# Gate's inner layer and logits, tile by tile in the stage before the gate

## The reference

```python
x = x + _L1_gnn_ref(xn, ...) + _L1_mix_ref(xn[None], ...)[0]          # attention over edges, token mix
x = x + _L1_ffn_ref(_layernorm(x, axis=-1)[None], L1_ffn_gw1, L1_ffn_gb1, L1_ffn_gw2, L1_ffn_gb2, ...)[0]
# the gate inside _L1_ffn_ref, for each row v of the normalised x:
#   hidden = relu(v @ gw1 + gb1)        512 -> 256
#   logits = hidden @ gw2 + gb2         256 -> 8
#   softmax over the 8, the 2 largest chosen and weighted; each row goes through its 2 experts (512 -> 1024 -> 512)
```

## Time and profile before

| | us |
|---|---|
| runs | 2231.5 median of 3, 2230.55 to 2233.77 |
| profiled execution | 2237.73, its span 2236.0 |
| PE busy in the span | 1948.7 (87%) |
| DVE busy | 1317.6 (59%) |
| POOL busy | 773.0 (35%) |
| ACT busy | 738.9 (33%) |
| mean granted clock of PE | 0.936 |

### The profile page before, as it was taken

How to read it: one execution, slowest core, us unless ns; L and a number is a source line. 1 busy time by engine, 2 the same in 40 slices (tenths; PEclk the granted TensorE clock), 3 DMA queues, 4 the chain that set the end, 5 groups by cost and what they waited for, 6 DMA issues and landing times. The chain is left out here.

```text
span 2236.0 us, 31082 instructions
## 1 busy us (share of the span) xinstructions
PE 1948.7 (87%) x10042; PEld 1082.3 (48%) x10043; DVE 1317.6 (59%) x3824; ACT 738.9 (33%) x1743; POOL 773.0 (35%) x849
## 2 busy tenths in 40 slices
PE   7998888988988988978769897699999884999997
PEld 4343433433433433433134453377777544777675
DVE  5883398898988988988753053176666423111111
ACT  0011244444444444443221130056666320222221
POOL 0000277777777777777700000011111000212211
PEclk9998998989999999999979898899999985999999
DMA  4001299999999999999930083355532142343451
GB/s 157 12 24 73 89 401 400 386 407 400 391 404 391 401 405 397 393 399 398 403 134 0 17 247 106 111 177 147 148 113 89 53 175 89 109 113 109 124 175 28
DMA packets 142939, 480.28 MB, mean 215 GB/s; under 512 B 16607, under 2 KB 17279, under 8 KB 142561
## 3 DMA queue, kind: packets, MB, share of 16 engines
q0 software_dynamic: 99952, 353.16, 41.9%
q1 hardware_dynamic: 42864, 125.60, 16.9%
HBM read 446.58 MB, written 32.11 MB: 214 GB/s over the span
## 5 line engine op out<-in xcount | busy, mean ns | idle before, releaser
L489 POOL DMA_INDIRECT m_ring<-in_table,m_rows_at x640 | 651.9, 1019 | 258.6 <-issue 144.1
L854 PE MATMUL m_acc<-m_ring,m_diag 64*64 64x512 f32 x2560 | 424.4, 675 | 129.5 <-ACT m_diag L663 129.5
L549 DVE CUSTOM_DVE_ANT_0 m_ring<-m_ring,m_coming,m_part 128x512 f32<-128x512 f32 x640 | 442.3, 747 | 43.0 <-DMA m_ring<-in_table,m_rows_at 33.5
L854 PEld LDWEIGHTS m_acc<-m_ring,m_diag 64*64 64x64 f32 x2560 | 136.1, 145 | 382.6 <-ACT m_diag L663 288.5
L663 ACT ACTIVATE m_diag<-m_eye,m_inner 128x64 f32<-128x64 f32 x640 | 222.3, 348 | 278.8 <-DVE m_inner L549 278.7
L1921 PEld LDWEIGHTS e_psU<-e_rowsT,x_w 128*128 128x128 f32 x1472 | 170.5, 194 | 14.2 <-issue 14.2
L1404 DVE CUSTOM_DVE_ANT_0 a_prob<-a_psS,xnT 128x1250 f32<-128x1250 f32 x80 | 116.8, 1460 | 102.3 <-PE a_psS L1341 102.3
L1921 PE MATMUL e_psU<-e_rowsT,x_w 128*128 128x128 f32 x1472 | 171.0, 278 | 3.0 <-DMA x_w<-in_we 1.9
L1930 PE MATMUL e_psY<-x_w,e_hT 128*128 128x512 f32 x368 | 161.7, 592 | 0.0
L1341 PE MATMUL a_psS<-a_k,a_q 128*128 128x512 f32 (+1 forms) x480 | 116.6, 379 | 20.7 <-DMA a_k<-qk_parts 16.3
L1327 POOL DMA_DIRECT2D a_q<-qk_parts x80 | 43.0, 539 | 257.5 <-PE a_psS L1341 257.1
(11 more groups left out here) (327 smaller groups left out, 2649.8 us busy)
## 6 DMA issues: line engine op xcount, KB each, us to landing
x_w<-in_we SPq DMA_DIRECT2D x16, 2048.0 KB, 11.0
xnT<-edge_log_counts SPq DMA_DIRECT2D x40, 640.0 KB, 3.9
m_ring<-in_table,m_rows_at POOLq DMA_INDIRECT x640, 6.7
qk_parts<-p_parts SPq DMA_DIRECT2D x32, 320.0 KB, 4.0
a_k<-qk_parts SPq DMA_DIRECT2D x32, 320.0 KB, 9.6
edge_log_counts<-p_log_cnt SPq DMA_DIRECT2D x10, 640.0 KB, 6.2
a_q<-qk_parts POOLq DMA_DIRECT2D x80, 64.0 KB, 2.1
edge_counts<-cnt SPq DMA_DIRECT2D x10, 320.0 KB, 2.1
```

The lines of the kernel that those rows point to most:

```text
L489: pool.indirect_dma_start(ring[:, slot, :], None, ins["table"], bass.IndirectOffsetOnAxis(rows_at[:, h, k:k + 1], 0)).then_inc(s_land[slot ...
L549: dve.tensor_tensor_reduce(ring[:, slot, 0:D], ring[:, slot, 0:D], coming[:, t % 2, :], part[:, b, k:k + 1], 0.0, ALU.mult, ALU.add, inner ...
L854: mm = pe.matmul(acc[to, i, :], diag[rows, h % 2 * TOPK + k, :], ring[rows, nth % RING, D:2 * D], start=h == 0 and k < 2, stop=h == HEADS ...
```

## The change

The gate's inner layer, its Relu, its logits and the addition of their bias move from the start of stage_gate into the loops of stage_join, one tile at a time: Relu(t-3) at the end of ACT's iteration t, logits(t-4) and hidden(t-3) at the end of PE's iteration t, the logits' bias of tile t-5 in DVE's iteration t, behind var and ahead of the rows. psG is now two halves of one tile and psL one tile of 8 columns, each a single buffer. `logit` is a tensor that outlives the join. stage_gate begins with the maximum. The renumbering of psL's parts in stage_gate and the passing on of `gate` and `logit` are left out below.

```diff
@@ stage_join, scalar
-            for t in range(NT + 2):
+            for t in range(NT + 3):
...
-                if t >= 2:
+                if 2 <= t < NT + 2:
                     act.wait_ge(s["norm_turned"], t - 1)
                     act.activation(c.xnT[:, :, (t - 2) * P:(t - 1) * P], psN[:, t % 2, :].rearrange("p (k n) -> p k n", k=KC),
                                    ACT.Copy).then_inc(s["norm_out"], 1)
+                if t >= 3:
+                    u = t - 3
+                    act.wait_ge(s["hidden"], u + 1)
+                    if u >= 2:
+                        act.wait_ge(s["logits"], u - 1)
+                    for m in range(2):
+                        act.activation(gT[:, u % 2, m, :], psG[:, m, :], ACT.Relu, bias=gb1[:, m:m + 1]).then_inc(s["relu"], 1)
@@ stage_join, tensor
+            def hidden(u):
+                if u == 0:
+                    pe.wait_ge(s["ahead"], 16 * len(ahead))
+                else:
+                    pe.wait_ge(s["relu"], 2 * u)
+                pe.wait_ge(s["norm_out"], u + 1)
+                for m in range(2):
+                    for k in range(KC):
+                        mm = pe.matmul(psG[:, m, :], gw1[:, k, m * P:(m + 1) * P], c.xnT[:, k, u * P:(u + 1) * P],
+                                       start=k == 0, stop=k == KC - 1)
+                mm.then_inc(s["hidden"], 1)
+
+            def logits(u):
+                pe.wait_ge(s["relu"], 2 * u + 2)
+                if u:
+                    pe.wait_ge(s["logit_out"], u)
+                for m in range(2):
+                    mm = pe.matmul(psL[:, :], gT[:, u % 2, m, :], gw2[:, m, :], start=m == 0, stop=m == 1)
+                mm.then_inc(s["logits"], 1)
+
             turn(0)
-            for t in range(NT + 2):
+            for t in range(NT + 4):
...
-                if t >= 2:
+                if 2 <= t < NT + 2:
...
+                if t >= 4:
+                    logits(t - 4)
+                if 3 <= t < NT + 3:
+                    hidden(t - 3)
@@ stage_join, vector
-            for t in range(NT + 1):
+            for t in range(NT + 5):
...
                     dve.tensor_scalar(var[:, t:t + 1], mv[:, t, 1:2], EPS, None, ALU.add).then_inc(s["var"], 1)
-                if t >= 1:
+                if t >= 5:
+                    dve.wait_ge(s["logits"], t - 4)
+                    dve.tensor_tensor(logit[:, t - 5, :], psL[:, :], gb2[:, :], ALU.add).then_inc(s["logit_out"], 1)
+                if 1 <= t <= NT:
@@ stage_gate, tensor
-            for m in range(2):
-                for i, (a, n) in enumerate(CHUNKS):
-                    u = 3 * m + i
-                    if u >= 2:
-                        pe.wait_ge(s["relu"], u - 1)
-                    for k in range(KC):
-                        mm = pe.matmul(psG[:, u % 2, 0:n], gw1[:, k, m * P:(m + 1) * P], c.xnT[:, k, a:a + n],
-                                       start=k == 0, stop=k == KC - 1)
-                    mm.then_inc(s["hidden"], 1)
-            pe.wait_ge(s["relu"], 6)
-            for t in range(NT):
-                for m in range(2):
-                    mm = pe.matmul(psL[:, 0, t, :], gT[:, m, t * P:(t + 1) * P], gw2[:, m, :], start=m == 0, stop=m == 1)
-            mm.then_inc(s["logits"], 1)
@@ stage_gate, scalar
-            for m in range(2):
-                for i, (a, n) in enumerate(CHUNKS):
-                    u = 3 * m + i
-                    act.wait_ge(s["hidden"], u + 1)
-                    act.activation(gT[:, m, a:a + n], psG[:, u % 2, 0:n], ACT.Relu, bias=gb1[:, m:m + 1]).then_inc(s["relu"], 1)
@@ stage_gate, vector
-            dve.wait_ge(s["logits"], 1)
-            dve.tensor_tensor(logit[:, :, :], psL[:, 0, :, :], gb2[:, :].unsqueeze(1).to_broadcast([P, NT, EXP]), ALU.add)
-            dve.drain()
```

More of the change, by code:

```diff
@@ L1479, in _, with stage_join @@
                 message(g, 0, 4)
-def stage_join(c, msg, weights, ahead):
+def stage_join(c, msg, weights, gate, ahead):
     nc = c.nc
@@ L1491, in stage_join @@
         stats, mv, var, root, rstd = sb("stats", [P, NT, 6]), sb("mv", [P, NT, 2]), sb("var", [P, NT]), sb("root", [P, NT]), sb("rstd", [P, NT])
+        gw1, gw2, gb1, gb2, logit = gate
+        gT = sb("gT", [P, 2, 2, P])
         psT, psO, psN = ps("psT", [P, 2, D]), ps("psO", [P, 2, D]), ps("psN", [P, 2, D])
+        psG, psL = ps("psG", [P, 2, P]), ps("psL", [P, EXP])
         s = {n: c.sem("j_" + n) for n in ("turned", "mT", "out", "sum_out", "var", "root", "rows", "norm_turned", "norm_out",
-                                          "saved0", "saved1", "started", "ahead")}
+                                          "hidden", "relu", "logits", "logit_out", "saved0", "saved1", "started", "ahead")}
         block = st.enter_context(nc.Block())
@@ L1580, in _, with stage_attention @@
                                       ALU.subtract, ALU.mult).then_inc(s["rows"], 1)
-def stage_attention(c, ahead):
+def stage_attention(c, gate, ahead):
     ins = c.ins
@@ L1605, in stage_attention @@
         c.end_stage()
-        stage_join(c, msg, join, ahead)
+        stage_join(c, msg, join, gate, ahead)
         c.end_stage()
@@ L1617, in rows_of, with stage_gate @@
     return P if t < NT - 1 else TAIL
-def stage_gate(c, route, weights, ahead):
+def stage_gate(c, route, logit, ahead):
     nc, ins = c.nc, c.ins
@@ L1631, in stage_gate @@
         ps = lambda n, s: st.enter_context(nc.psum_tensor("r_" + n, s, F32))
-        gw1, gw2, gb1, gb2 = weights
-        gT = sb("gT", [P, 2, NP])
-        logit, expo, gate = sb("logit", [P, NT, EXP]), sb("expo", [P, NT, EXP]), sb("gate", [P, NT, EXP])
+        expo, gate = sb("expo", [P, NT, EXP]), sb("gate", [P, NT, EXP])
         peak, total, top, top_at = sb("peak", [P, NT]), sb("total", [P, NT]), sb("top", [P, NT, 8]), sb("top_at", [P, NT, 8], U32)
@@ L1649, in stage_gate @@
         hot_lane, hot_block = sb("hot_lane", [P, 2, NT, P]), sb("hot_block", [P, CHOICES, 2, NT, BLOCKS])
-        psG, psL, psK = ps("psG", [P, 2, D]), ps("psL", [P, 3, NT, EXP]), ps("psK", [P, 2, BLOCKS])
-        s = {n: c.sem("r_" + n) for n in ("iota", "number", "hidden", "relu", "logits", "shifted", "exp", "gap", "exp2",
+        psL, psK = ps("psL", [P, 2, NT, EXP]), ps("psK", [P, 2, BLOCKS])
+        s = {n: c.sem("r_" + n) for n in ("iota", "number", "shifted", "exp", "gap", "exp2",
                                           "tri", "both", "member", "ranked", "hot_block", "hot_lane", "listed", "blank", "blanked",
@@ L1693, in _ @@
         def _(pe):
-            for m in range(2):
-                for i, (a, n) in enumerate(CHUNKS):
-                    u = 3 * m + i
-                    if u >= 2:
-                        pe.wait_ge(s["relu"], u - 1)
-                    for k in range(KC):
-                        mm = pe.matmul(psG[:, u % 2, 0:n], gw1[:, k, m * P:(m + 1) * P], c.xnT[:, k, a:a + n],
-                                       start=k == 0, stop=k == KC - 1)
-                    mm.then_inc(s["hidden"], 1)
-            pe.wait_ge(s["relu"], 6)
-            for t in range(NT):
-                for m in range(2):
-                    mm = pe.matmul(psL[:, 0, t, :], gT[:, m, t * P:(t + 1) * P], gw2[:, m, :], start=m == 0, stop=m == 1)
-            mm.then_inc(s["logits"], 1)
             pe.wait_ge(s["tri"], 1)
             pe.wait_ge(s["member"], 1)
-            pe.matmul(psL[:, 1, :, :], below[:, :], member[:, :, :], start=True, stop=True)
-            pe.matmul(psL[:, 2, :, :], ones[:, :], member[:, :, :], start=True, stop=True).then_inc(s["ranked"], 1)
+            pe.matmul(psL[:, 0, :, :], below[:, :], member[:, :, :], start=True, stop=True)
+            pe.matmul(psL[:, 1, :, :], ones[:, :], member[:, :, :], start=True, stop=True).then_inc(s["ranked"], 1)
             pe.wait_ge(s["hot_block"], 1)
@@ L1771, in _ @@
             dve.wait_ge(s["ranked"], 1)
-            dve.tensor_copy(tally[:, :, :], psL[:, 2, :, :])
+            dve.tensor_copy(tally[:, :, :], psL[:, 1, :, :])
             dve.memset(before[:, 0, :], 0.0)
@@ L1795, in _ @@
             dve.tensor_scalar(base[:, :], start[:, 0:EXP], float(P), None, ALU.mult)
-            dve.tensor_tensor(rank[:, :, :], psL[:, 1, :, :], before[:, 0:NT, :], ALU.add)
+            dve.tensor_tensor(rank[:, :, :], psL[:, 0, :, :], before[:, 0:NT, :], ALU.add)
             dve.drain()
@@ L1972, in gate_weights, with stage_experts @@
     sb = lambda n, s: st.enter_context(c.nc.sbuf_tensor("x_" + n, s, F32))
-    gate = sb("gw1", [P, KC, 2 * P]), sb("gw2", [P, 2, EXP]), sb("gb1", [P, 2]), sb("gb2", [P, EXP])
-    gw1, gw2, gb1, gb2 = gate
+    gate = sb("gw1", [P, KC, 2 * P]), sb("gw2", [P, 2, EXP]), sb("gb1", [P, 2]), sb("gb2", [P, EXP]), sb("logit", [P, NT, EXP])
+    gw1, gw2, gb1, gb2, logit = gate
     return gate, [(gw1[:, :, :], chunked(ins["gw1"])), (gw2[:, :, :], chunked(ins["gw2"])), (gb1[:, :], ins["gb1T"]),
                   (gb2[:, :], ins["gb2"].partition_broadcast(P))]
-def stage_experts(c, gate):
```

(7 more changed lines are left out.)

## The result

The changed kernel takes 2240.4 us (median of 7 runs, 2235.4 to 2245.1). The kernel before takes 2231.5 (7 runs, the three named above among them, 2228.9 to 2235.6). The ratio is 1.0039, with a 95% interval from 1.0024 to 1.0054: slower, by 5 to 12 us. The forecast was 2242.

The account below looks back on a forecast made before the run. PE was taken as the join's busiest engine. At full clock 22.4 us added less 27.5 removed gave -5.1; clock falls of +12 and +4 made +10.9 on 2231.5, so 2242 us, range 2236 to 2248 (chance 0.66).

Parts of the forecast that it names:

- The wait: In the join, PE waits some 2.5 us ahead of the logits of tiles 1 to 5, released by DVE's logit add.
- The gate: At the gate's start, 28.8 us ahead of Exp shrink to 1.3 us for the table load: 27.5 us removed.
- The weight loads: In the gate, SP's last large weight load lands 19.8 us behind the stage's start, still 11 us early.
- The added products: In each join tile, eight hidden and two logit matmuls on PE at 0.11 us each: 0.88 and 0.22 us.
- t=3 and t=4: Join tiles without a wait for the logit add: +0.9 and +1.1 us.
- a stalled tile: Join tiles t=5 to 8, where PE waits for the add: 9.23 us instead of 5.38, +3.85 each at full clock.
- the end: End of the join, three rounds of Relu, logits, hidden at 2.09 us each: +5.0 us, plus 4 for low clock.
- The clock: In the join, PE's clock falls in four stalled tiles, 3.0 us each, +12, and stays low at the end, +4.
- the clock holds: Rival, chance 0.12: PE's clock doesn't fall in the join despite 2.55 us idle; -5.1 us, 2226 us, faster.
- The sum: Whole kernel: 22.4 us added at full clock, 27.5 removed, then 12 and 4 for the clock: +10.9 us.

Follow-up runs that it names:

- experiment 1: Changed kernel with the logit add of tile t-5 moved to the head of DVE's iteration t: 2224.8 us, ratio 0.9970.
- experiment 6: Changed kernel with the tile's `bn_stats` repeated between `var` and the logit add in five DVE iterations: 2258.9 us, one run.
- experiment 4: Changed kernel with ACT's Relu of tile t-4 behind mT(t), the logit add left behind `var`: 2238.8 us, ratio 1.0043.
- experiment 5: Changed kernel with ACT's Relu of tile t-4 behind mT(t) and eleven unused identity matmuls in PE's idle time: 2229.6 us, ratio 0.9997.
- experiment 3: Changed kernel with eleven unused identity matmuls in PE's idle time ahead of the logits of tiles 1 to 5: 2235.5 us, ratio 1.0025.
- experiment 7: Changed kernel with the logit add first, Relu behind the next mT, and a one-column Exp ending ACT's work in the join: 2214.5 us, one run.

## Why the prediction was right, and which terms were not

- **The wait: right, in place and size.** PE idles 2.55 ahead of the logits of tiles 1 to 5, released by the add. Experiments 1 and 6 show that the add's place behind the chain is the cause.
- **The gate: right.** Exp 1.3 behind the start, the stage 27.5 shorter (58.36 less 30.86). The further drain that the Trainium skill counts on top of a table load ("ScalarE: Activation LUTs", "What ACT_TABLE_LOAD costs") isn't in this trace: load at 1850.71, Exp at 1852.01. The weight loads didn't end late: they were through 19.3 behind the start, where I had 19.8.
- **The added products: mis-sized by half.** "Eight hidden matmuls" and "two logit matmuls" a tile were counted from the calls in the code. PE issues 16 and 4: an f32 product is two instructions. The rows of before had it: 40 logit instructions for 20 calls, psO x8 for four k. The price of one, 0.11, was right. So t=3 and t=4 cost 1.80 and 2.26 instead of 0.9 and 1.1, a stalled tile at full clock 5.04 (t=7, 10.42) instead of 3.85, and a round of the end 3.21 instead of 2.09, hence 9.6 instead of 5.0. In all 33.8 instead of 22.4.
- **The clock: right in kind, mis-sized the other way.** Against the 10.42 of t=7, the others lost 0.97, 1.63 and 2.67: 5.3 in three tiles, where I took 12 in four. What a fall costs depends on what it lies over: in t=6 on the hidden products (3.66 us instead of 2.03 in t=7), in t=8 mostly on psO (5.90 instead of 3.67). My 3.0 for each was above all three. The end kept 1.00, where I took 4 for it. The rival "the clock holds" was right for one tile and for the end.
- **The sum.** 33.8 + 5.3 = 39.1 added, against 22.4 + 16 = 38.4. That the forecast is so close is luck: two errors of 11 us cancel. The signs and the mechanism stand, the sizes of these two terms don't. Had the count been right and the clock term kept, the forecast would have been 11 us later, at 2254, outside the range.

## What to carry to other kernels

When a step moves into a software-pipelined loop, look on each engine for what now stands ahead of the instruction that frees its buffer: the read of a single PSUM buffer goes to the head of the iteration, not behind a chain that used to be covered. Count PE's instructions in the trace, not the calls in the code. Where a wait opens a gap on PE, read the granted clock tile by tile: the gap may cost again as a lower clock, and that can hide what another edit gains (experiments 4 and 5).

## What the hardware showed that was not expected

- More work on PE made the join shorter. With 22 instructions whose result is never read in the idle time of each stalled tile, the clock stayed at 1.00 and the join was 5.6 and 11.2 us shorter (experiments 3 and 5). Between experiments 4 and 5 the times show it too: ratios of 1.0043 and 0.9997, with intervals that don't overlap.
- An idle time of 2.55 us, followed by the same products, brought the clock down in three of four tiles of the changed kernel and in four of four of experiment 4; 3.50 us did so in four of four of experiment 6. The same logits without the idle time left it at 1.00 (experiment 1). Why tile t=7 of the changed kernel kept 1.00, and why the end kept it there and not in experiment 4, isn't settled by these runs.
- The same instructions behind the same idle time can go either way. PE stands 1.83 us at the barrier ahead of the join in all nine kernels, and its first 5.5 us there hold the same work; the granted clock was 1.00 in three profiled executions (before, experiments 3 and 7) and 0.69 in the six others.
